# Attention over 200,000 edges: eight short comparisons for one wide, their order, and where a buffer is filled

## The reference

```python
    xp = (x @ W).reshape(N, H, C)
    a_src = jnp.einsum('nhc,hc->nh', xp, att_src)
    a_dst = jnp.einsum('nhc,hc->nh', xp, att_dst)
    e = jax.nn.leaky_relu(a_src[src] + a_dst[dst], NEG_SLOPE)
    m = jax.ops.segment_max(e, dst, num_segments=N)
    ex = jnp.exp(e - m[dst])
    denom = jax.ops.segment_sum(ex, dst, num_segments=N)
    alpha = ex / (denom[dst] + 1e-16)
    msg = xp[src] * alpha[:, :, None]
    out = jax.ops.segment_sum(msg, dst, num_segments=N).reshape(N, H * C)
```

## Time and profile before

| | |
|---|---|
| median of three runs | 9468.76 us |
| lowest, highest | 9463.22, 9489.17 us |
| the profiled execution's own time | 9472.64 us |
| its span, first to last instruction | 9470.8 us |
| TensorE busy | 7599.4 us (80%) |
| VectorE busy | 6462.5 us (68%) |
| GpSimd busy | 5787.9 us (61%) |
| ScalarE busy | 2902.1 us (31%) |
| granted TensorE clock, mean | 0.85 |

### The profile page before, as it was taken

One profiled execution on the slowest core, in us unless ns is written; L12 is line 12 of the kernel. 1 busy time (PEld: TensorE's weight loads), 2 busy tenths in 40 slices (PEclk: granted clock), 3 DMA queues, 4 the chain that ended last, 5 costly groups with the idle time before them and its releaser, 6 DMA issues. The chain is left out here.

```text
span 9470.8 us, 285464 instructions
## 1 busy us (share of the span) xinstructions
PE 7599.4 (80%) x87223; PEld 6468.6 (68%) x87223; DVE 6462.5 (68%) x21922; ACT 2902.1 (31%) x8008; POOL 5787.9 (61%) x5766
## 2 busy tenths in 40 slices
PE   4887999998999996899999957999945666666662
PEld 4886999996999995466666646787834555555552
DVE  7997777775777776677777766676764555555556
ACT  3884222223222224322222242122241222222222
POOL 2663777773777772166666624666625777777771
PEclk7998999999999997999999978999976566655665
DMA  2002666664666665633333335555532222222223
GB/s 63 28 27 72 157 161 154 155 158 135 153 154 151 152 155 168 220 92 87 90 87 88 88 103 146 135 142 139 140 104 74 65 66 66 66 66 67 67 66 102
DMA packets 1057653, 1044.16 MB, mean 110 GB/s; under 512 B 171994, under 2 KB 957065, under 8 KB 1056897
## 3 DMA queue, kind: packets, MB, share of 16 engines
q1 hardware_dynamic: 869802, 654.88, 24.9%
q0 software_dynamic: 174080, 369.69, 16.8%
q10 hardware_dynamic: 13399, 16.26, 0.5%
HBM read 877.56 MB, written 169.10 MB: 111 GB/s over the span
## 5 line engine op out<-in xcount | busy, mean ns | idle before, releaser
L1048 DVE TENSOR_SCALAR state<-iota_row,state 128x128 f32<-128x128 f32 x5488 | 1444.4, 374 | 0.0
L1561 POOL DMA_INDIRECT state<-rel_table,state x1120 | 1065.2, 951 | 504.9 <-issue 323.1
L1107 PE MATMUL psum<-ring 128*128 128x128 bf16 x21276 | 1275.5, 221 | 58.1 <-DVE ring L1041 58.1
L1107 PEld LDWEIGHTS psum<-ring 128*128 128x128 bf16 x21276 | 1208.2, 99 | 109.8 <-issue 42.5
L1027 POOL DMA_INDIRECT ring<-rows,idx x980 | 957.5, 977 | 368.6 <-issue 327.7
L1027 POOL DMA_INDIRECT ring<-gcn_table,idx x980 | 957.5, 977 | 352.6 <-issue 324.8
L2612 POOL DMA_INDIRECT acc<-att_table,acc x896 | 935.0, 1043 | 273.1 <-issue 263.6
L1276 POOL DMA_INDIRECT state<-hyp_table,state x784 | 751.4, 958 | 419.5 <-issue 217.8
L2612 POOL DMA_INDIRECT ring<-att_table,acc x672 | 698.0, 1039 | 441.4 <-ACT acc L2654 245.4
L1122 PE MATMUL psum<-state 64*128 64x128 f32 x14112 | 958.7, 278 | 0.0
L1041 DVE TENSOR_SCALAR ring<-sel,iota_col 128x640 bf16<-128x640 bf16 (+1 forms) x1576 | 513.4, 369 | 600.3 <-PE psum L1107 581.6
(11 more groups left out here) (444 smaller groups left out, 14711.7 us busy)
## 6 DMA issues: line engine op xcount, KB each, us to landing
ring<-xparts SPq DMA_DIRECT2D x1332, 192.0 KB
ring<-srow SPq DMA_DIRECT2D x544, 128.0 KB
sel<-drow SPq DMA_DIRECT2D x394, 160.0 KB
sel<-drow SPq DMA_DIRECT2D x394, 128.0 KB
rel_table<-tout SPq DMA_DIRECT2D x98, 512.0 KB, 2.6
ring<-rows SPq DMA_DIRECT2D x56, 448.0 KB
xparts<-state SPq DMA_DIRECT2D x28, 672.0 KB, 3.6
rows<-acc SPq DMA_DIRECT2D x42, 448.0 KB
```

The lines of the kernel that those rows point to most:

```text
L1048: ins = nc.vector.tensor_scalar(picks[u][:, j, :], iota_row[:, :], tabS[:, bass.ds(n * SJ + j, 1)], tabW[:, bass.ds(n * SJ + j, 1)], ALU.i ...
L1107: last = nc.tensor.matmul(rowsP[v][:, j * P:(j + 1) * P], reach[v][:, t, j * P:(j + 1) * P], xwin[u][:, t, i, :], start=(t + i == 0), stop ...
L1561: pool.indirect_dma_start(out=type_rows[j % RB][:, k, :], out_offset=None, in_=table, in_offset=bass.IndirectOffsetOnAxis(ap=type_idx[j % ...
```

## The change

There are three edits. (1) `select` makes its 128x1024 matrix with eight TENSOR_SCALARs of 128x128, each with its own column of `dstrel` as a per-partition operand, in place of one TENSOR_TENSOR with two broadcast inputs. (2) In VectorE's step `select` stands ahead of `scan`, and `scan` is followed by a wait for its own end. (3) `body` is filled in the sort's loop, in 49 pieces of 256 rows and one of 128, from SyncE's queue, out of a row that now lies in `rown` and is written once in the setup; the first cell pass fills nothing. (`starts8`, a table in memory that nothing used, is gone too.)

```diff
-        no_sums = sq[:, 0:ROW7]
+        no_sums = rown[:, 0:2, :].rearrange("p a t -> p (a t)")[:, 0:ROW7]
...
+                c(nc.vector.memset(no_sums[:, 0:ME], 0.0))
+                c(nc.vector.memset(no_sums[:, ME:ROW7], -BIG))
...
+                    def clear_rows(j):
+                        at = j * (PT * P)
+                        sp.dma_start(body[bass.ds(at, PT * P), :].rearrange("(t p) c -> p t c", p=P),
+                                     no_sums.unsqueeze(1).to_broadcast([P, PT, ROW7])
+                                     ).then_inc(sem("kept1"), 16)
+
...
                             keep(it * 2 + v)
                             load(it * 2 + (v + 2), v)
+                            clear_rows(it * 2 + v)
                     keep(PIECES - 3)
+                    for j in range(PIECES // 2 * 2 - 2, PIECES):
+                        clear_rows(j)
+                    sp.dma_start(body[PIECES * PT * P:NPAD, :].rearrange("(t p) c -> p t c", p=P),
+                                 no_sums.unsqueeze(1).to_broadcast([P, NPAD // P - PIECES * PT, ROW7])
+                                 ).then_inc(sem("kept1"), 16)
...
-                    if table is rows0:
-                        sp.wait_ge(sem("made"), 1)
-                        sp.dma_start(body[SG * SUMS:NPAD, :].rearrange("(t p) c -> p t c", p=P),
...
-                        if table is rows0:
-                            sp.dma_start(body[bass.ds(sg * SUMS, SUMS), :].rearrange("(t p) c -> p t c", p=P),
...
-                    if table is rows0:
-                        nc.vector.memset(no_sums[:, ME:ROW7], -BIG)
-                        nc.vector.memset(no_sums[:, 0:ME], 0.0).then_inc(sem("made"), 1)
...
                             nc.vector.tensor_tensor_scan(runmax, starts_T[w], sT, -BIG, ALU.add, ALU.max
                                                          ).then_inc(sem("runmax"), 1)
+                            dve.wait_ge(sem("runmax"), n + 1)
...
-                            nc.vector.tensor_tensor(
-                                sel_of[w], iota_row[:, :].unsqueeze(1).to_broadcast([P, K, P]),
-                                dstrel[:, bass.ds(n * K, K)].unsqueeze(2).to_broadcast([P, K, P]),
-                                ALU.is_equal).then_inc(sem("selected"), 1)
+                            for k in range(K):
+                                ins = nc.vector.tensor_scalar(sel_of[w][:, k, :], iota_row[:, :],
+                                                              dstrel[:, bass.ds(n * K + k, 1)], None,
+                                                              ALU.is_equal)
+                            ins.then_inc(sem("selected"), 1)
...
+                        select(i)
                         scan(i)
-                        select(i)
```

More of the change, by code:

```diff
@@ L119, in gnn_kernel @@
         att_table = nc.dram_tensor("att_table", (NPAD, ROW6), F32, kind="Internal").ap()
-        starts8 = nc.dram_tensor("starts8", (EC * HEADS, P), F32, kind="Internal").ap()
         startrow = nc.dram_tensor("startrow", (EC, P), F32, kind="Internal").ap()
@@ L705, in _ @@
                     sp.wait_ge(sem("xin1"), PIECES // 2 * 16)
+                    sp.wait_ge(sem("kept1"), PIECES * 16 + 16)
                 @block.tensor
@@ L996, in load @@
                                      ).then_inc(sem(f"din{u}"), 16)
-                    if table is rows0:
-                        sp.wait_ge(sem("made"), 1)
-                        sp.dma_start(body[SG * SUMS:NPAD, :].rearrange("(t p) c -> p t c", p=P),
-                                     no_sums.unsqueeze(1).to_broadcast([P, (NPAD - SG * SUMS) // P, ROW7])
-                                     ).then_inc(sem("kept1"), 16)
                     with sp.Fori(0, SG) as sg:
-                        if table is rows0:
-                            sp.dma_start(body[bass.ds(sg * SUMS, SUMS), :].rearrange("(t p) c -> p t c", p=P),
-                                         no_sums.unsqueeze(1).to_broadcast([P, SUMS // P, ROW7])
-                                         ).then_inc(sem("kept1"), 16)
                         with sp.Fori(0, IT) as it:
@@ L1010, in _ @@
                                 load(sg * GB + it * 4 + u, it * 4 + u, u)
-                    if table is rows0:
-                        sp.wait_ge(sem("kept1"), (SG + 1) * 16)
                     for u in range(4):
```

## The result

The changed kernel takes 9341.34 us (median of four runs, 9332.5 to 9343.6) beside 9465.99 us for the kernel before on the same chip: a ratio of 0.9864, 95% interval 0.9844 to 0.9884. Faster, as forecast, but by 125 us (1.3%) where 79 to 83 were expected.

A forecast was written before the change was run, and what follows sets the result against it. GpSimd's issuing of indirect gathers was taken to bound the attention pass. Terms -69 + 1 - 15 + 0.4 = -83 us against 9472.6 gave 9390 us; range 9340 to 9460, the forecast's own bounds 9348 to 9447.

The forecast's parts named there:

- The bound: Attention pass: GpSimd's issuing of 1568 indirect gathers sets the time, at least 9.99 us a group; other engines run in its shadow.
- The comparison's term (-69): Attention pass: eight short comparisons for one wide return GpSimd issue time, -69 us, bounds 27 and 110.
- net 0.35 us: Attention pass, per group: 0.40 us returned by the wide comparison less 0.05 for the short ones, times 196 groups.
- the random 0.57: Attention pass: us a group the wide comparison would hold issues if issues and comparisons met at random.
- the bound of 110: Attention pass: the most the comparison edit was to gain, 0.56 us a group over 196 groups, 110 us.
- Order and wait: 0: Attention pass: comparisons ahead of the scan plus VectorE's wait fit into 4.8 us of idle time; 0, +1 at the pass's end.
- the short comparisons lock GpSimd out: Rival, attention pass: short comparisons act as a chain that never lets the issue in; +0.9 us a group, about 9630; chance 0.08.
- One tensor input doesn't hold: Attention pass: VectorE operations with one tensor input don't stretch gather issues, read from the typed and first cell passes.
- The cell pass: First cell pass: without the body fill it becomes as long as the second, -15 us, bounds 0 and 16.
- The fill in the sort: Sort: 50 added fill DMAs go into SyncE's 10.4 us waits, cost 0; rival that it isn't hidden, +20 us, chance 0.08.
- The stall moves on: Rival, attention pass: held issues meet the messages or small two-input operations instead, pass keeps its time; 9457, chance 0.14.
- All of it comes back: Rival, attention pass: the messages' stalls hang on the comparison's phase and go too; -0.7 us a group, 9320, chance 0.08.

The follow-up runs named there:

- eight with two inputs: Changed kernel with its eight short comparisons as TENSOR_TENSORs of 128x128, both inputs in SBUF: 9532.9 us, attention pass 2216.5.
- fill-alone kernel: Kernel before with only the body fill moved into the sort's loop, attention pass as before: 9458.1 us, attention pass 2153.0.
- Edit 1 alone: Kernel before with eight short comparisons for the wide one, behind the scan, no added wait, fill as before: 9467.6 us beside 9482.2, ratio 0.9982.
- The wide one: Changed kernel with one TENSOR_SCALAR of 128x1024, one tensor input, in place of the eight short comparisons: 9372.8 us, attention pass 2067.1.

## Why the prediction was right and wrong

**The bound** was right. The pass moved with the mean issue in every kernel; what is left of it without the 1568 issues is 518 to 521 us in all seventeen traces: 113.1 us less of issuing made a pass 112.6 us shorter, and 64.2 us more of it (eight with two inputs: 955.9 + 741.3 against 1633.0) made it 64.6 longer. VectorE's longer comparisons cost nothing: its wait for the transpose shrank by 1.1 us a group.

**The comparison's term (-69) failed.** The step is "net 0.35 us": a share of 0.40 for the wide comparison, 0.05 for the short ones wherever they stand, and no change elsewhere. By its parts: the wide one's share was 96.6/196 = 0.49, between the 0.40 taken and the random 0.57; the short ones cost 5.6/196 = 0.03 in the changed kernel, as in the rows of the typed pass; and the untouched L2744 and messages went from 56.3 to 32.8 us, another 0.12, which the prediction had at nothing (as a rival it had all of it). 0.49 - 0.03 + 0.12 = 0.58 us, 114 over the pass, beside 112.6 measured: just past the bound of 110. By the split of the fill-alone kernel the same sum is 0.56 - 0.03 + 0.06: then the wide one stands at the random value and the untouched ones gave half as much. Either way the 0.40 was too small, and this much is a term with the wrong size. The group that it leaned on (0.19) was one of 196.

**"Order and wait: 0" was wrong in kind.** I priced them by VectorE's time and not by what they do to GpSimd. Edit 1 alone, which the text gave -69, brought 6.1: it is the rival "the short comparisons lock GpSimd out", at 0.58 us a group in place of that rival's 1.3, the size of the wide one's hold, in the place behind the scan. The changed kernel escapes it only because they stand elsewhere, or because the wait is there: 103.6 us for the one wait. That the sum of the terms for the pass, -68, was still of the right sign was luck in this respect: it put the whole gain on an edit that brings 6 us alone, and nothing on the one that lets it work. I had the row for it (the comparison starts 0.08 us before the scan's end) and used it for the wait's price alone. The typed pass, my evidence that short ones are harmless, has no scan ahead of them (there they follow a TENSOR_SCALAR, L1582).

**"One tensor input doesn't hold"** was wrong as a rule and right as a number. The wide one holds an issue to its end (1.43 us); the short ones hold it too, but only until the one that is running ends (at most 0.13 us in the changed kernel and wherever no scan, copy or MEMSET was put directly ahead of them). I had one-input rows of short instructions only.

**The cell pass**: -15 forecast, -15.6 measured, and -16.2 with the fill alone. The mechanism is right; that the two agree within 1 us is partly luck, as the pass with its fill took 1324.8 to 1331.7 us. **The fill in the sort**: 0 forecast; the stage is 678 to 685 us in all kernels here, with the fill or without, 679.2 before and 678.2 after. Its 49 issues take SyncE's 18 us, in waits that were 10.4 us a step.

**Rivals.** "The stall moves on" is refuted (the messages' share rose from 17.2 to 21.5 us, but L2744's fell from 39.1 to 11.3). "All of it comes back" is half true at most: 23.5 of 56 us came back from untouched instructions, or 12.7 of 45.5 by the other trace of the same pass.

**Open.** Why a run of short one-input comparisons directly behind a scan keeps issues out, why these are then let in at points that are no instruction's end, and why a MEMSET between takes away a part of the loss and not all. The kernels here narrow it to what stands directly ahead of the run; that the small differences in spacing are the cause and not another sign of it is only argued. It isn't two inputs ahead of it either: in the changed kernel without the wait the run stands behind L2744's operation, which has two inputs and no gap behind it, and holds 10.0 us.

## What to carry to other kernels

Where GpSimd's indirect gathers are the clock of a stage, read how long one issue takes beside its own minimum, and find VectorE's instruction that ends a fixed time before the long ones end: that instruction is the price, however idle VectorE is. Split it into short operations with one tensor input, and then look again at what they stand behind, for the same eight instructions cost 113 us directly behind a scan and 6 to 10 in the other places or behind a wait. Two edits that measure near nothing or worse alone (-6, +14) can be worth 113 together, so test the pair before either is dropped.

## What was not expected of the hardware

A TENSOR_SCALAR of 128x1024 holds a GpSimd gather's issue until it ends (1.43 us in place of 0.94), as a TENSOR_TENSOR does. Eight TENSOR_TENSORs of 128x128 hold it through all eight (2.82 us); eight TENSOR_SCALARs of the same size let it in at the next end (1.01), except directly behind a TENSOR_TENSOR_SCAN, where one whose point fell 0.39 us into the run took 2.18, to the run's end. A wait of VectorE for its own scan, 0.24 us of idle time, ended that.
